# Where a dense step of a product-key attention puts the rank sums of the next chunk pair

## The reference

```python
h = _L0_tok_ref(x, ..., stride=2)            # 4 tanh layers, 15-tap pooling: 375 frames
h = h + _L0_attn_ref(_layernorm(h), ...)     # forward and backward GRU, gate, output layer
h = h + _L0_ffn_ref(_layernorm(h), ...)      # product-key memory attention
```

```python
scores, idx = jax.lax.top_k(sim, PK_TOPK)                 # two lists of 64 keys each
score = scores[0][..., :, None] + scores[1][..., None, :] # 256 sums, best 16 kept
final_scores, pk_idx = jax.lax.top_k(score, FINAL_TOPK)
final_scores = jax.nn.softmax(final_scores, axis=-1)
k = jnp.einsum('bnhk,bnhkd->bnhd', kv_scores, keys_table[ind])
v = jnp.einsum('bnhk,bnhkd->bnhd', kv_scores, values_table[ind])
attn = jax.nn.softmax(where(causal, einsum(q, k), neg)); out = (attn @ v) @ Wo
```

## Time and profile before

| | us |
|---|---|
| median of 3 runs | 7287.46 (7281.98 to 7302.77) |
| the profiled execution | 7299.86 |
| its span, first to last instruction | 7298.1 |
| first dense exponent to the last product (the last stage) | 1396 to 7234 |
| one middle batch, the ninth (first `w` to the first `w` of the next) | about 371 |

### The profile page before, as it was taken

The page is one execution under the profiler, slowest core; times in us unless marked ns, Lnnn a source line. Parts: engine busy times, 40 slices in busy tenths (PEclk is TensorE's granted clock), DMA queues, the critical chain, the costliest instruction groups (busy, mean ns, idle before and its releaser), DMA issues.

```text
span 7298.1 us, 100450 instructions
## 1 busy us (share of the span) xinstructions
PE 5621.8 (77%) x27362; PEld 3684.4 (50%) x27362; DVE 4393.5 (60%) x17472; ACT 2245.5 (31%) x5708; POOL 3077.3 (42%) x3041
## 2 busy tenths in 40 slices
PE   4677774378878888888787877787887788878789
PEld 2577761144545555555555554454554555555556
DVE  6555556575656575756575757565666565756522
ACT  2322221123333333333332333333333333323233
POOL 0000000454645455545555555454555455554541
PEclk7555556678787888888888787878887887878787
DMA  1000001122211222121212121212121212121220
GB/s 32 0 0 0 0 0 43 42 57 59 61 56 54 60 58 62 56 63 54 60 56 60 56 60 53 59 56 59 54 65 54 58 57 59 57 59 56 59 59 25
DMA packets 157825, 353.56 MB, mean 48 GB/s; under 512 B 71716, under 2 KB 75812, under 8 KB 156968
## 3 DMA queue, kind: packets, MB, share of 16 engines
q0 software_dynamic: 96912, 200.25, 10.5%
q1 hardware_dynamic: 60440, 147.74, 6.2%
HBM read 345.04 MB, written 4.61 MB: 48 GB/s over the span
## 4 chain that ended last, share of the span: by engine, by line
PE 36%; another core or an unknown queue 19%; DVE 13%; issue 11%; ACT 4%; DVEq 0%; DMA 0%; ACTq 0%; POOLq 0%
PE ps L928 36%; DVE w L1509 2%; DVE topi L1323 2%; ACT ex L1186 1%; DVE top L1317 1%; DVE sc L1329 1%; DVE idxf L1485 1%; DVE left L1287 1%; DVE hot L1481 1%; DVE hot L1476 0%; ACT L1186 0%; DVE eq L1446 0%; DVE eq L1454 0%; DVE wmat L1501 0%
## 5 line engine op out<-in xcount | busy, mean ns | idle before, releaser
L920 POOL DMA_INDIRECT rows<-table_dram,idxT x3024 | 3069.8, 1015 | 2913.8 <-PE ps L928 1704.8
L1509 DVE SCALAR_TENSOR_TENSOR w<-ps,ex 128x750 f32<-128x750 f32 x1024 | 958.0, 936 | 1920.6 <-remote 831.8
L928 PE MATMUL ps<-w,dtab 128*128 128x375 f32 x4096 | 1824.5, 576 | 16.6 <-issue 16.4
L928 PEld LDWEIGHTS ps<-w,dtab 128*128 128x128 f32 x4096 | 910.9, 229 | 489.2 <-issue 257.7
L1186 ACT ACTIVATE ex<-ps 128x750 f32<-128x750 f32 x1024 | 818.2, 799 | 747.7 <-PE ps L928 366.3
L928 PEld LDWEIGHTS ps<-wmat,rows 128*128 128x128 f32 x6048 | 788.2, 206 | 158.9 <-issue 118.5
L928 PE MATMUL ps<-wmat,rows 128*128 128x8 f32 x6048 | 790.4, 264 | 77.6 <-issue 68.0
L928 PE MATMUL ps<-rank_dense,half 128*128 128x375 bf16 x1920 | 539.9, 367 | 391.8 <-DVE w L1509 308.9
L928 PE MATMUL ps<-parts,half 128*128 128x375 bf16 x2048 | 607.1, 372 | 246.3 <-ACT ex L1186 170.5
L928 PEld LDWEIGHTS ps<-rank_dense,half 128*128 128x128 bf16 x1920 | 188.4, 109 | 906.3 <-DVE w L1509 468.5
L928 PE MATMUL ps<-dg,prob 125*125 125x125 f32 x1536 | 319.7, 341 | 267.1 <-DVE wmat L1501 111.3
(11 more groups left out here) (209 smaller groups left out, 8066.8 us busy)
## 6 DMA issues: line engine op xcount, KB each, us to landing
dtab<-dense_dram SPq DMA_DIRECT2D x256, 512.0 KB
rows<-table_dram,idxT POOLq DMA_INDIRECT x3024
xin<-x_dram SPq DMA_DIRECT2D x16, 187.5 KB
half<-halves_dram POOLq DMA_DIRECT2D x1, 1828.0 KB, 13.1
rows_in<-hh SPq DMA_DIRECT2D x16, 93.8 KB, 2.2
rows_in<-uu SPq DMA_DIRECT2D x16, 93.8 KB, 2.2
u_front<-rows_in SPq DMA_DIRECT2D x16, 93.8 KB
h_now<-rows_in SPq DMA_DIRECT2D x16, 93.8 KB
```

What stands on the lines that cost most here:

```text
L920: nc.gpsimd.indirect_dma_start(out=rows[:, t, :], out_offset=None, in_=table[:, :], in_offset=bass.IndirectOffsetOnAxis(ap=idxT[:, c, t:t ...
L928: return nc.tensor.matmul(out_, lhsT, rhs, start=start, stop=stop, skip_group_check=open_bank)
L1509: nc.vector.scalar_tensor_tensor(w[:, p % 2, :, :], ps[:, 2:4, 0:T], float(K), ex[:, p % 2, :, :], ALU.is_gt, ALU.mult).then_inc(s_w, 1)
```

## The change

In `step` of TensorE, the call `ranks(*following)`, which makes the rank sums of the next pair, stands behind the loop over the step's small units (`sim`, `query`, `value`, `turn_probs`, `part`, `eat`) and no longer between `product` and that loop. `weigh` and the front units follow as before. Nothing else is edited; the waits inside each call go with it.

```diff
                 if p == 0 and kind != "first":
                     product(n - 1, STEPS - 1)
-                if dense:
-                    ranks(*following)
                 for name, i in here(0, p, kind) + here(1, p, kind):
                     if name == "sim":
                         sim(i, kind, n)
...
                     if name == "eat":
                         gathered(i, kind, n)
+                if dense:
+                    ranks(*following)
                 for m in items(TURN_AT, p - 1, kind):
                     weigh(m, kind, n)
```

## The result

The changed kernel takes 7557.22 us (median of 4 runs, 7535.09 to 7572.32), the kernel before beside it 7284.72 us. The ratio is 1.0384, with a 95% interval of 1.0348 to 1.0420: 272 us slower, where I had forecast no change (7297 us) and a range up to 7380.

The account below looks back on a forecast made before the run. TensorE was taken to set the pace outside five late-result stretches a batch, VectorE following with a quarter free. Gain 45 us and loss 55 us gave +10 us, 7297 us for the median; range 7215 to 7380 us.

Parts of the forecast that it names:

- In a TensorE-paced stretch the delay of `w` costs nothing: Outside the five idle stretches: `w` about 2.1 us later costs nothing, as work between successive rank sums stays the same.
- The example that I chose: Ninth-batch stretch 4482 to 4517 us, TensorE 96% and VectorE 86% busy, shown as typical of TensorE setting the pace.
- step 16: Ninth-batch example: rank sums and `w` of pair 17 come about 2.1 us later, yet TensorE has no gap.
- The gain term: TensorE's waits for `w` ahead of the rank sums: 68 of 136 us filled with units, two thirds taken, 45 us gained.
- The cost term: TensorE's 23 waits for `wmat` each 2.1 us longer, 48 us, plus 7 us for masks: 55 us lost.
- Inside the five stretches, zero: Five late-result stretches, 113 us of the ninth batch: filling waits there nets zero, at most 67 us gained.
- nothing in the rows ties it to the place of the rank sums: TensorE's late results, 831.8 us of VectorE's idle time ahead of `w`, were seen as not tied to the order.
- remote: Idle time ended by a semaphore no record explains; to stay near 830 us, a move by hundreds meaning the prediction wrong.
- (1): Rival: VectorE starves and is the bound; one part in five of 456 us, 91 us slower, 7378 us; chance 0.26.
- (3): Rival: TensorE's clock falls as narrow `eat` matmuls come between wide ones; 113 us slower, 7400 us; chance 0.05.
- (2): Rival: TensorE's waits are filled without cost at `wmat`; 102 us faster, 7185 at best, likelier 7220 us; chance 0.27.
- (4): Rival: bank waits hold the units until `w` is done, nothing gets ahead; forecast's time, counted with it, together 0.42.

Follow-up runs that it names:

- the kernel with only ready units in front: Changed kernel, but rank sums stand before the step's first unit whose bank VectorE empties behind this step's `w`; 5987.69 us against 5783.07 for the kernel before.
- the lighter VectorE: Front's `eq` and `hot` operations cut to 8 of 64 keys and 8 of 50 candidates; with gathers 7396.96 us in the order before, 7614.56 us changed.
- the pair without gathers: Orders before and changed, each indirect DMA replaced by a one-column memset; 5784.28 and 6042.42 us, on another chip 5792.05 and 6070.07 us.
- the light pair: Orders before and changed, both with `eq` and `hot` cut to 8 keys and 8 candidates and without gathers; 5596.59 and 5664.04 us.

## Why the prediction was wrong

**The failing step** is "In a TensorE-paced stretch the delay of `w` costs nothing". It rested on VectorE following "with a quarter of its time free", taken as a mean over a batch. Where no result is late, the runs show that the delay does cost: the kernel with only ready units in front waits no longer for masks (1.3 us) and little longer for `left` and `wmat` (34.6 and 43.5 us, after 32.2 and 35.4), and loses 205 us; the lighter VectorE takes the loss of the changed order from 278 to 67 us. For fifty steps of a batch VectorE is 92% busy. The example that I chose had it at 86% and without a gap; I noted that and gave it to a rival. In step 16 itself the reasoning held; I took one step for all. On the chip of the result, with its late results, the lighter VectorE took only about 60 us away, so there the cause of the 272 us is in part open.

**The gain term** had the right direction and was too small as a wait: TensorE's wait for `w` fell by 182 us, from 309.2 to 127.5 (68 us were to be filled, less than 200 to be left), in the pair without gathers by 94 us. No 45 us came of it at the end, for the waits for the banks grew by more.

**The cost term** was put at the wrong place. `wmat` was to cost 48 us and measured 18.7 more (153.6 to 172.3); the masks, "taken as 7 us", measured 289 more (8.5 to 297.3), and `left`, with no term at all, 96.5. I had counted the held units as units that can't fill the wait, and not as units that now stand between `w` and the rank sums.

**"Inside the five stretches, zero"** and **"nothing in the rows ties it to the place of the rank sums"**: whether the first holds stays open. The loss is 272 and 278 us with late results and 258 and 278 without, but beside the lighter VectorE 214 and 218 with and 67 without. The second does not hold: "remote" ahead of `w` went from 831.8 to 1260.7 us, as the text had named for its own failure. The late results come from the gathers, and their sum depends on the order; the order loses without them too.

**The rivals.** (1), VectorE starves, is what happened where no result is late, with its condition (`w` to `w` on VectorE longer than TensorE's step, for several steps on end). Its price, 91 us, came from one part in five reaching the end; without gathers it is 278 of 350 us, four in five. (3), the clock, came with it: TensorE's busy time rose by 72 us, and by 103 in the stage without gathers, near the 113 of that rival, and in the kernel with ready units in front the longer matmuls are more than half of the loss. The mechanism was another, though. Narrow matmuls between wide ones don't suffice to lower the clock: the same order keeps 0.94 beside the lighter VectorE, with 37 us *less* busy time. The fall comes with a full VectorE, but which waits make it, or whether it makes waits in turn, wasn't tried. The Trainium skill ("TensorE: Matmul & The Clock Gate", HAM oscillation) puts the falling clock down to TensorE's gaps; the trace agrees in the pair with a full VectorE, 0.93 to 0.91 with 172 us more idle time, and the light pair shows no fall though idle time rose from 99 to 199 us. (2) and (4) did not happen.

**The range** ended at 7380, since (1) stood in it with one part in five of its own 456 us. With the full price the upper end would have been about 7740.

## What to carry to other kernels

Where two engines work in turns through a single buffer, let as little as can be stand between the release and the next hand-over. Work put there to fill a wait adds its own waits to the turn, and even work that is ready delays the hand-over: here that alone cost 205 us, since the other engine had no time to catch up. Judge the other engine's spare time over the steps concerned, not over a period that has a quiet end: here 84% over a batch (228.9 of 273 us) was 92% in fifty steps in a row. And before an edit is costed, look for time that belongs to nothing recorded; here it hid that two engines were nearly full, and it still keeps open how the 272 us are made up.

## What the runs showed of the hardware

Indirect DMAs from GpSimd, 3024 of 128 rows, cost 1506 us of 7298 on one chip and nothing on another, in the same program. On the first kind, ScalarE stands idle for up to 19.0 us ahead of a result of TensorE's, until a semaphore moves that no record explains. Plain copies of the same size, queue and semaphore leave no such trace on a chip of that kind. The Trainium skill ("DMA: Bandwidth & Descriptors", SWDGE vs HWDGE vs iDMA) says that GpSimd writes the descriptors of its DMAs to rings in SBUF, and that VectorE locks it out of that memory while it runs in a 2-port mode. No run here bears that out as the cause: the plain copies take the same queue undisturbed, and a VectorE with less work made the disturbed kernel 60 and 115 us slower. Gathering with fewer instructions was not measured.
